# A recommendation tower on one core: a sixth selected field, a gather ring of 13 rows, and a reordered head

## The reference

```
e = jnp.stack([tbl_0[ids[:, 0]], ..., tbl_31[ids[:, 31]]], axis=1)
z = einsum('bnd,bmd->bnm', e, e)[:, iu, ju]
h = concatenate([z, dense_ctx], axis=1)
h = maximum(h @ W_top1 + b_top1, 0)      # 512 -> 512
h = maximum(h @ W_top2 + b_top2, 0)      # 512 -> 256
y = h @ W_top3                           # 256 -> 1
```

## Time and profile before

| | us |
|---|---|
| median of 3 runs | 585.84 |
| lowest and highest run | 584.89 and 585.88 |
| the profiled execution, its own time | 583.17 |
| its span in the trace | 581.1 |

### The profile page before, as it was taken

How to read it: one execution, slowest core, us unless ns; L and a number is a source line. 1 busy time by engine, 2 the same in 40 slices (tenths; PEclk the granted TensorE clock), 3 DMA queues, 4 the chain that set the end, 5 groups by cost and what they waited for, 6 DMA issues and landing times.

```text
span 581.1 us, 16242 instructions
## 1 busy us (share of the span) xinstructions
PE 503.9 (87%) x7108; PEld 479.1 (82%) x7108; DVE 360.5 (62%) x747; ACT 263.8 (45%) x390; POOL 419.8 (72%) x440
## 2 busy tenths in 40 slices
PE   0266679999999999999999999999999999997786
PEld 0266679898989989898989899898989898996685
DVE  1334467676757577658667677657767675754543
ACT  0223255454546255444636345544645445533542
POOL 6777777777777777777777777777777777777710
PEclk9997799999999999999999999999999999998799
DMA  5999434444433444434443443444443443433310
GB/s 132 257 253 241 108 98 116 115 118 122 117 116 105 127 115 116 119 111 127 115 115 111 120 120 113 115 119 121 118 117 106 133 117 105 119 102 109 105 35 0
DMA packets 35595, 70.15 MB, mean 121 GB/s; under 512 B 13107, under 2 KB 18627, under 8 KB 35527
## 3 DMA queue, kind: packets, MB, share of 16 engines
q0 software_dynamic: 20832, 56.91, 35.1%
q1 hardware_dynamic: 14695, 12.22, 8.9%
HBM read 69.09 MB, written 0.01 MB: 119 GB/s over the span
## 4 chain that ended last, share of the span: by engine, by line
PE 40%; POOL 35%; issue 12%; DVE 5%; ACT 4%; DMA 2%; POOLq 0%; DVEq 0%
POOL rows L318 35%; PE sel_ps L416 15%; PE gram_ps L356 9%; PE tr_ps L332 7%; PE gram_ps L378 4%; DMA rows<-in_tbl,ids_sb 2%; PE gram_ps L388 2%; DVE sel_low L614 2%; ACT sel_high L769 1%; DVE onehot L631 1%; ACT emb_t L537 1%; DVE emb_t L537 1%; ACT emb_t L545 1%; PE gram_ps L396 1%; PE sel_ps L356 1%
## 5 line engine op out<-in xcount | busy, mean ns | idle before, releaser
L318 POOL DMA_INDIRECT rows<-in_tbl,ids_sb x434 | 419.1, 966 | 134.4 <-issue 129.8
L416 PE MATMUL sel_ps<-onehot,sel_high 125*128 125x256 f32 x624 | 164.6, 301 | 24.8 <-DVE sel_low L614 22.6
L537 ACT COPY emb_t<-tr_ps 128x512 f32<-128x512 f32 (+1 forms) x112 | 124.3, 1114 | 100.9 <-PE tr_ps L332 99.9
L416 PE MATMUL sel_ps<-onehot,sel_low 125*128 125x256 f32 x624 | 158.8, 291 | 0.0
L416 PEld LDWEIGHTS sel_ps<-onehot,sel_high 125*128 125x128 f32 x624 | 124.9, 200 | 30.4 <-DVE sel_low L614 23.8
L332 PE MATMUL tr_ps<-ident,rows 128*128 128x128 f32 x868 | 117.5, 279 | 33.2 <-DMA rows<-in_tbl,ids_sb 25.6
L537 DVE COPY emb_t<-tr_ps 128x512 f32<-128x512 f32 (+1 forms) x112 | 120.4, 1086 | 29.0 <-PE tr_ps L332 28.1
L332 PEld LDWEIGHTS tr_ps<-ident,rows 128*128 128x128 f32 x868 | 98.4, 143 | 38.7 <-issue 29.4
L356 PEld LDWEIGHTS gram_ps<-emb_t 128*64 128x64 f32 x3840 | 116.9, 139 | 15.3 <-issue 12.0
L356 PE MATMUL gram_ps<-emb_t 128*64 128x62 f32 x3840 | 121.8, 224 | 8.4 <-ACT emb_t L537 5.6
L416 PEld LDWEIGHTS sel_ps<-onehot,sel_low 125*128 125x128 f32 x624 | 125.1, 200 | 0.0
(11 more groups left out here) (48 smaller groups left out, 157.6 us busy)
## 6 DMA issues: line engine op xcount, KB each, us to landing
rows<-in_tbl,ids_sb POOLq DMA_INDIRECT x434
sel_raw<-in_tbl SPq DMA_DIRECT2D x5, 896.0 KB
sel_ids<-in_ids_by_field SPq DMA_DIRECT2D x35, 128.0 KB
w_sb<-in_W_top SPq DMA_DIRECT2D x1, 1024.0 KB, 22.8
sel_raw<-in_tbl SPq DMA_DIRECT2D x5, 104.0 KB
dots_t<-in_ids_by_field SPq DMA_DIRECT2D x4, 128.0 KB, 5.8
w_sb<-in_W_top SPq DMA_DIRECT2D x1, 512.0 KB, 27.0
ids_sb<-in_ids SPq DMA_DIRECT2D x1, 240.0 KB, 3.1
```

The costliest lines, as they stand in the source:

```text
L318: pool.indirect_dma_start(out=rows[:, slot, :], out_offset=None, in_=tables[f], in_offset=bass.IndirectOffsetOnAxis(ap=ids_sb[:, t, f:f + ...
L416: last = nc.tensor.matmul(sel_ps[j % 2][:, h, :], table[:, i, c, h * P:(h + 1) * P], onehot[:, c, :], start=(c == 0 and table is sel_high) ...
L537: copy(emb_t[t % PAIR][:, h, :, at[0]:at[-1] + 1].rearrange("p (g s) f -> p f s g", s=QUAD), tr_ps[h][g % 2][:, 0:len(at), :].rearrange("p ...
```

## The change

Field 19 joins the selected fields; they are six now. The ring has 13 slots, not 28. Two selected fields are gathered in pair 0, so the head keeps its four jobs, and tiles 0 and 1 still gather 28 rows; all other tiles gather 26. The list of jobs is written with a tuple of how many fields each pair gathers. The tables load in the order of their use: the four of the head, then the two of pair 1. In the head, ScalarE casts and VectorE splits a table one job earlier than before, and VectorE builds the one-hot of pair 1's first job ahead of the copy of the last quad. In `last_periods`, the third layer of tile 14 moves behind the first layer of tile 15 on TensorE, and VectorE's copies move with it.

```diff
-SELECTED = (20, 22, 24, 27, 31)
+SELECTED = (19, 20, 22, 24, 27, 31)
-RING = 28
+RING = 13
-GATHERED_FIRST = 1
+GATHERED = (2, 0, 0, 0, 0, 0, 0, 0)
...
     def n_gathered(t):
-        return n_rows + (GATHERED_FIRST if t < PAIR else 0)
+        return n_rows + GATHERED[t // PAIR]
...
     def jobs(t):
-        p, at = (t + 1) // PAIR, range(0, EARLY) if t % PAIR else range(EARLY, n_sel)
-        if t == 0:
-            at = range(GATHERED_FIRST, n_sel)
-        return [(p, i) for i in at] if p < tiles // PAIR else []
+        p = (t + 1) // PAIR
+        if p >= tiles // PAIR:
+            return []
+        own = [(p, i) for i in range(GATHERED[p], n_sel)]
+        return own if t == 0 else own[:EARLY] if t % PAIR else own[EARLY:]
...
+    def table_place(i):
+        return (i - GATHERED[0]) % n_sel
...
-            for n in range(GATHERED_FIRST, n_sel):
-                load_table(n)
-            for n in range(GATHERED_FIRST):
+            for n in sorted(range(n_sel), key=table_place):
                 load_table(n)
...
                 layer2(t - 1)
-                layer3(t - 1)
                 turn(t)
                 layer1(t)
+                layer3(t - 1)
                 layer2(t)
                 layer3(t)
...
                 turn_dots(t)
+                turn_copy(dve, 0, copy, t)
                 layer2_copy(dve, 0, bias_relu, t - 1)
+                layer1_copy(dve, 0, bias_relu, t)
                 y_copy(t - 1)
-                turn_copy(dve, 0, copy, t)
-                layer1_copy(dve, 0, bias_relu, t)
                 layer2_copy(dve, 0, bias_relu, t)
                 y_copy(t)
...
-            for g in range(quads):
-                emb_copy(dve, 0, copy, g)
-                if g in SELECT_AFTER:
-                    split_table(SELECT_AFTER.index(g))
-                    job = next(next_jobs)
-                    for half in range(2):
-                        build_onehot(job, half)
-            for n in range(n_sel - GATHERED_FIRST, n_sel):
-                split_table(n)
+            emb_copy(dve, 0, copy, 0)
+            emb_copy(dve, 0, copy, 1)
+            split_table(0)
+            split_table(1)
+            for half in range(2):
+                build_onehot(first_jobs[1], half)
+            emb_copy(dve, 0, copy, 2)
+            split_table(2)
+            for half in range(2):
+                build_onehot(first_jobs[2], half)
+            emb_copy(dve, 0, copy, 3)
+            emb_copy(dve, 0, copy, 4)
+            split_table(3)
+            for half in range(2):
+                build_onehot(first_jobs[3], half)
+            emb_copy(dve, 0, copy, 5)
+            split_table(4)
+            for half in range(2):
+                build_onehot(first_jobs[4], half)
+            emb_copy(dve, 0, copy, 6)
+            for at in range(5, n_sel):
+                split_table(at)
...
-                if g in SELECT_AFTER:
-                    high_table(SELECT_AFTER.index(g))
-                    copy_selected(0, next(first_jobs))
+            emb_copy(act, 1, copy, 0)
+            emb_copy(act, 1, copy, 1)
+            high_table(0)
+            high_table(1)
+            copy_selected(0, first_jobs[0])
+            emb_copy(act, 1, copy, 2)
+            high_table(2)
+            copy_selected(0, first_jobs[1])
+            emb_copy(act, 1, copy, 3)
+            emb_copy(act, 1, copy, 4)
+            high_table(3)
+            copy_selected(0, first_jobs[2])
+            emb_copy(act, 1, copy, 5)
+            high_table(4)
+            copy_selected(0, first_jobs[3])
+            emb_copy(act, 1, copy, 6)
+            for at in range(5, n_sel):
+                high_table(at)
```

More of the change, by code:

```diff
@@ L78, in n_gathered @@
     def n_gathered(t):
-        return n_rows + (GATHERED_FIRST if t < PAIR else 0)
+        return n_rows + GATHERED[t // PAIR]
     rows_before = [sum(n_gathered(i) for i in range(t)) for t in range(tiles)]
-    assert n_gathered(0) <= quads * QUAD
+    assert len(GATHERED) == tiles // PAIR and max(GATHERED) == GATHERED[0] <= quads * QUAD - n_rows
     def places(t, k):
@@ L103, in jobs @@
     def jobs(t):
-        p, at = (t + 1) // PAIR, range(0, EARLY) if t % PAIR else range(EARLY, n_sel)
-        if t == 0:
-            at = range(GATHERED_FIRST, n_sel)
-        return [(p, i) for i in at] if p < tiles // PAIR else []
+        p = (t + 1) // PAIR
[3 more added lines that the diff above has]
+        return own if t == 0 else own[:EARLY] if t % PAIR else own[EARLY:]
+    jobs_before = [sum(n_sel - GATHERED[q] for q in range(p)) for p in range(tiles // PAIR + 1)]
     def job_number(p, i):
-        return p * n_sel + i - GATHERED_FIRST
+        return jobs_before[p] + i - GATHERED[p]
     def ids_loads(p, i):
-        first, j = n_sel - GATHERED_FIRST, job_number(p, i)
-        return len(range(j % 2 + (first if (first - j) % 2 == 0 else first + 1) - j % 2, j + 1, 2))
+        j = job_number(p, i)
+        return len([n for n in range(jobs_before[1], j + 1) if n % 2 == j % 2])
     def jobs_in_bank(bank, p):
-        return len(range(bank, (p + 1) * n_sel - GATHERED_FIRST, 2))
-    turns_odd, turns_even = quads - 1, quads + 1
+        return len(range(bank, jobs_before[p + 1], 2))
+    def table_place(i):
+        return (i - GATHERED[0]) % n_sel
     def quad_turned(t, at):
@@ L194, in ids_of @@
         def ids_of(p, i):
-            return first_ids[:, i - GATHERED_FIRST, :] if p == 0 else sel_ids[job_number(p, i) % 2][:]
+            return first_ids[:, i - GATHERED[0], :] if p == 0 else sel_ids[job_number(p, i) % 2][:]
         onehot = sbuf("onehot", [select_rows, SELECT_CHUNKS, pair_cols], f32r)
@@ L406, in select @@
                 if h == 0:
-                    if p < 2:
-                        pe.wait_ge(tables_split, (i - GATHERED_FIRST) % n_sel + 1)
+                    if i < GATHERED[0] or p == 0:
+                        pe.wait_ge(tables_split, table_place(i) + 1)
                     for u in range(PAIR):
@@ L516, in _ @@
             pe.wait_ge(ident_ready, 1)
-            first_jobs = iter(jobs(0))
+            first_jobs = jobs(0)
             for g in range(quads):
@@ L521, in _ @@
                 if g in SELECT_AFTER:
-                    job = next(first_jobs)
                     for h in range(D_HALVES):
-                        select(job, h)
+                        select(first_jobs[SELECT_AFTER.index(g)], h)
             for t in range(1, last_tile, PAIR):
@@ L610, in split_table @@
             def split_table(at):
-                n = (at + GATHERED_FIRST) % n_sel
+                n = (at + GATHERED[0]) % n_sel
                 dve.wait_ge(tables_high, at + 1)
@@ L731, in last_periods @@
                 turn_dots(t)
+                turn_copy(dve, 0, copy, t)
                 layer2_copy(dve, 0, bias_relu, t - 1)
+                layer1_copy(dve, 0, bias_relu, t)
                 y_copy(t - 1)
-                turn_copy(dve, 0, copy, t)
-                layer1_copy(dve, 0, bias_relu, t)
                 layer2_copy(dve, 0, bias_relu, t)
                 y_copy(t)
-            first_jobs = jobs(0)
-            next_jobs = iter(first_jobs[1:] + jobs(1)[:1])
+            first_jobs = jobs(0) + jobs(1)[:1]
             for half in range(2):
                 build_onehot(first_jobs[0], half)
-            for g in range(quads):
-                emb_copy(dve, 0, copy, g)
-                if g in SELECT_AFTER:
-                    split_table(SELECT_AFTER.index(g))
-                    job = next(next_jobs)
-                    for half in range(2):
-                        build_onehot(job, half)
-            for n in range(n_sel - GATHERED_FIRST, n_sel):
-                split_table(n)
+            emb_copy(dve, 0, copy, 0)
[20 more added lines that the diff above has]
+                split_table(at)
             dve.wait_ge(weights_loaded, 5 * DMA)
@@ L856, in last_periods @@
                 layer2_copy(act, 1, bias_relu, t)
-            first_jobs = iter(jobs(0))
-            for g in range(quads):
-                emb_copy(act, 1, copy, g)
-                if g in SELECT_AFTER:
-                    high_table(SELECT_AFTER.index(g))
-                    copy_selected(0, next(first_jobs))
-            for n in range(n_sel - GATHERED_FIRST, n_sel):
-                high_table(n)
+            first_jobs = jobs(0)
+            emb_copy(act, 1, copy, 0)
[16 more added lines that the diff above has]
+                high_table(at)
             act.wait_ge(weights_loaded, 5 * DMA)
```

## The result

The changed kernel takes **581.68 us** (median of 20 runs, 578.84 to 585.61), the kernel before 584.98 (20 runs, 583.61 to 586.89). The ratio is 0.9944, 95% interval 0.9930 to 0.9958: faster by 0.56%, 3.3 us. The profiled execution of the changed kernel took 583.61 us, with a span of 581.8.

A forecast was written before the change was run, and what follows sets the result against it. TensorE was taken to set the pace, 3.3 us a pair faster than the gathers and living on the ring's lead. Terms summed to -1.1 us on 581.1: 580.0, 582.1 profiled, 584.7 us with 2.7 added for the median; range 577 to 590.5.

The forecast's parts named there:

- The pairs: Middle pairs of tiles: 64.2 us plus 2.40 at the even end, less 0.35 at the odd end, giving 66.25 us.
- Rival 3: Even ends: the new selection keeps its full price, 3.65 us, +1.25 seven times, 593.5 us in all; chance 0.06.
- The ring: 13 gathered rows cost nothing in the pairs, where gathers have 1.25 us to spare; +0.4 us in the last periods.
- The head: Before the first pair: three split waits go, first Gram product at 65.4 us instead of 74.90, -9.5 us.
- The shift: Head: later arrival of pair 1's ids, a sixth table (3.8 us) against fewer gathers (-3.4 us), taken as +2.1 us.
- rival 2: Head: ids later, no gathers saved (+1.7 us) and landing 5.8 us instead of 2.7 (+3.1), 589.5 us; chance 0.12.
- rival 1: Head: ids come early, splits bound it at 59.2 us, another -6.2, 578.5 us (576 if clock stays up); chance 0.20.
- The clock: After the head's idle of some 9 us TensorE restarts at a granted clock of 0.50: +2.4 us after 65.4.
- The last periods and the tail: Last periods: row waits go, -4.6 us, and a slow Gram product, -1.5; tail: last tile's transposes start earlier, -0.9.
- The 1.2 us that I had held back: Part of the 5.8 us of late row waits, left out as already counted in the seventh even end, leaving -4.6.
- rival 4: Pairs: one-hot operations hold up GpSimd, 52 gathers take 68.0 us, six pairs +10.5 us, 595 us; chance 0.04.
- Rival 5: Head: the reordering gains nothing, since table loads hold the casts, 594 us; chance 0.03.

The follow-up runs named there:

- the two further executions: The changed kernel executed twice more with nothing edited: 579.96 us and 582.65 us.
- the lighter selection: Changed kernel with the sixth selection of each pair from pair 1 on doing 8 of its 32 matmuls: 575.78 us, ratio 0.9850 to the kernel before.
- the old head: Changed kernel with the head's casts and splits back in their old order on ScalarE and VectorE: 588.81 us, ratio 1.0065 to the kernel before.

## Why the prediction was right, and where it was not

The sign and the range came out: -1.1 us forecast, -3.3 measured. The gain is three times the forecast one, but both are what is left of far larger terms: some 17 us that seven selections cost, and some 20 that the head, the odd ends and the last periods gave back.

**The pairs.** Forecast 66.25; the six pairs of the two further executions take 66.31 and 66.28 each. Those of the first take 66.61, a hair over the 66.6 that was to mean wrong; without the wait on issue they would take 66.4. In the middle pairs of the further executions the even part (second Gram product of an even period to the next odd period) went from a mean of 30.25 us to 32.65 (+2.40, as forecast), and the odd part (last Gram product of an odd period to the first of the even one) fell from 19.09 to 18.77 (-0.32, forecast -0.35). Rival 3, a selection at full price, would have given 67.5: it fell.

**The ring.** Right: no wait for rows in the middle, with 13 rows or with 10. But the 1.25 us that GpSimd has to spare are all there is, as the lighter selection shows.

**The head.** The first Gram product was forecast at 65.4 and came at 65.54, 64.80 and 65.99. Two steps behind the number were wrong and cancelled. "The shift lies between +0.4 and +3.8; I take +2.1": it was -0.4, since the short ring gave 4.5 us, of which the forecast had put in about half of 3.4, and the rest of the change, with the sixth table in it, took 4.1. And the landing of 2.7 us was taken from a bias load of 1 KB, while a load of the same 128 KB of ids stood in the same group with 5.8; measured 5.52. The nearest row by time was not the nearest row by kind. So rival 2 had its landing and rival 1 its early queue, and that 65.4 was met is luck. What rival 1 promised was real: with the ids there in time the kernel takes 7.7 us less, somewhat over its 6.2.

**The clock.** After 11.86 us of idle the first Gram product took 3.68 us at a granted clock of 0.50, that is 1.2 GHz, in this window:

```profile
65.00:70.00 5.00, 4.46 (x68) 4.34 (x69) 3.23 (x4) 0.00 (x0) 0.00 (x0) 0.50 0.22 56
```

The stretch to the next Gram product is 7.12 to 7.43 us, 5.0 in the middle pairs: +2.1 to +2.4, and the forecast had 2.4.

**The last periods and the tail.** The 1.2 us that I had held back were rightly held back: at the seventh even end a wait for rows of 2.52 us stood in place of the 1.18, 1.34 more, and 2.40 less 1.34 is what that even part grew by (31.44 us before, 32.4 and 32.5 after). From the last odd period to tile 15's Gram product it took 29.5 us before and 23.7 after, so 5.8 less. The forecast comes to 4.8 less there: 3.3 of row waits, 1.5 of slow product and 0.35 of the last odd end, plus 0.4 of new waits. No new wait came. And the clock, put down as a mere chance, held in part behind the wait for the packed dots: the transposes and layer 1 there took 7.5 us at a mean granted clock of 0.63 before and 6.55 at 0.74 after, in these two windows:

```profile
547.40:555.00 7.60, 7.51 (x44) 7.54 (x45) 2.05 (x4) 1.38 (x2) 5.68 (x6) 0.63 0.38 106
```

```profile
550.80:557.35 6.55, 6.55 (x45) 6.55 (x46) 2.05 (x4) 1.39 (x2) 3.58 (x4) 0.74 0.34 100
```

The wait itself grew by 0.4. The tail gave 0.85, forecast 0.9.

**The step that failed** is the last: "against the median the forecast is 584.7". The span was forecast at 580.0, 582.1 us for a profiled execution; the three profiled ones took 583.61, 579.96 and 582.65, 582.1 on the average, and the median is 581.68. So the sum over the rows was met and the number given was 3.0 too high. Adding the 2.7 us by which the first profile lay under its median carried that execution's luck over to the changed kernel. Of the 1.3 us between two executions of that kernel 0.8 came with late rows, which the change removes, and the median of 20 runs of the kernel before is itself 0.9 lower than that of the three.

**The other rivals.** Gathers held up by one-hots (rival 4) did not come: 951 ns. The Trainium skill (SBUF — State Buffer, Who interferes with whom) says that a tensor_scalar can take the pair of ports that VectorE shares with GpSimd. No gather here is held up that way: the 90 of the changed kernel that start during a one-hot take 0.96 us on the average and 1.07 at most. Rival 5, a reorder that gains nothing, fell by the 7.1 us of the old head.

## What to carry over

When two engines share the bound, price the change for each of them by pair and then at both ends: here the middle could only lose, and the 3.3 us came from the head and the last periods. Take a missing duration from the row of the same kind and size, not from the neighbour in time, and ask of each load on a shared queue what is wanted first: two small id loads ahead of two tables were worth 7.7 us more. Don't add one execution's distance from the median to a forecast.

## What the runs showed that I had not expected

A gather that runs beside a table's split takes longer. The changed kernel's head, GpSimd first and VectorE's split after it:

```profile
45.58 2.42 POOL L321 DMA_INDIRECT rows<-in_tbl,ids_sb  x1 [0.30 <-issue]
48.31 0.95 POOL L321 DMA_INDIRECT rows<-in_tbl,ids_sb  x1 [0.30 <-issue]
```

```profile
44.91 2.27 DVE L616 TENSOR_TENSOR sel_low<-sel_raw,sel_high 125x2048 fp32r<-125x2048 f32 x1
```

The gather at 45.58 takes 2.42 us and the split runs from 44.91 to 47.18; the next gather, beside a one-hot, takes 0.95. The Trainium skill (SBUF — State Buffer, Who interferes with whom) says that a VectorE instruction with two inputs in SBUF contends with a GpSimd instruction that reads SBUF; a gather reads its ids there, and the trace agrees, at 1.1 to 1.8 us a split. It happens in the head alone, five times, and five times in the kernel before, where such a gather takes 2.11 to 2.98 us. That TensorE can wait 0.66 to 1.36 us inside a Gram product in one execution and not in the next, and at places that recur, and that its clock can fall over the tail's short waits in another, was new to me too; each is worth more than some terms of the sum.
